# Two mixture-of-experts stages of a four-stage block: from every expert for every token to two experts per token, in blocks of 256 rows

## The reference, cut to what matters

```python
x = x + A(layernorm(x))   # linear attention: 16 heads of 8, a decayed scan over the tokens
x = x + B(layernorm(x))   # mixture: 8 experts of 352 hidden rows, the best 2 per token
x = x + C(layernorm(x))   # selective scan over the tokens, 16 states per feature
x = x + D(layernorm(x))   # mixture: 8 experts of 128 rows, best 2, and 2 shared experts
```

```python
out = sum over e of gate[t, e] * (silu(x @ W1[e].T) * (x @ W3[e].T)) @ W2[e].T
```

## Time and profile before

| | |
|---|---|
| median of 3 runs | 2572.25 us (2572.23 to 2573.89) |
| the profiled execution | 2568.12 us |
| its span, first to last instruction | 2566.3 us |
| mean granted TensorE clock | 0.907 of full speed |
| instructions | 22885 |
| DMA | 17.70 MB, mean 7 GB/s |

### The profile page before, as it was taken

How to read it: one execution, slowest core, us unless ns; L and a number is a source line. 1 busy time by engine, 2 the same in 40 slices (tenths; PEclk the granted TensorE clock), 3 DMA queues, 4 the chain that set the end, 5 groups by cost and what they waited for, 6 DMA issues and landing times.

```text
span 2566.3 us, 22885 instructions
## 1 busy us (share of the span) xinstructions
PE 2075.6 (81%) x6944; PEld 862.4 (34%) x6944; DVE 1855.6 (72%) x3076; ACT 1134.1 (44%) x1491; POOL 1347.3 (52%) x848
## 2 busy tenths in 40 slices
PE   3589787889788887799887997788877998787478
PEld 1234333334333343334333343333432433332023
DVE  5655569776796859867697767968598676974972
ACT  1133375335644275343752347442653437535324
POOL 4346347553573537735485445835377353862343
PEclk9789898899888999899988999889998999988579
DMA  4000000000000000000000000000000000000000
GB/s 131 0 9 1 9 1 1 0 1 17 0 1 0 1 17 1 0 1 1 17 0 1 1 11 7 1 1 1 17 1 1 1 1 9 1 0 1 0 0 17
DMA packets 24876, 17.70 MB, mean 7 GB/s; under 512 B 2705, under 2 KB 23985, under 8 KB 24497
## 3 DMA queue, kind: packets, MB, share of 16 engines
q1 hardware_dynamic: 24752, 16.23, 2.1%
HBM read 12.04 MB, written 4.19 MB: 6 GB/s over the span
## 4 chain that ended last, share of the span: by engine, by line
PE 42%; issue 20%; DVE 17%; POOL 13%; ACT 7%; DMA 0%; DVEq 0%; POOLq 0%; SPq 0%; ACTq 0%
PE bank L920 9%; PE bank L780 7%; POOL mix_arena L746 6%; PE bank L782 6%; PE bank L781 6%; POOL y L727 4%; DVE arena L1247 3%; DVE arena L1303 3%; PE bank L843 3%; PE bank L908 2%; PE bank L824 2%; PE bank L791 2%; DVE arena L1314 2%; POOL arena L717 2%; DVE w L1320 1%
## 5 line engine op out<-in xcount | busy, mean ns | idle before, releaser
L746 POOL TENSOR_TENSOR mix_arena<-mix_arena 128x512 f32<-128x512 f32 (+1 forms) x512 | 815.4, 1608 | 689.3 <-ACT mix_arena L1100 688.4
L1388 DVE SCALAR_TENSOR_TENSOR mix_arena<-bank,winv,mix_arena 128x512 f32<-128x512 f32 (+1 forms) x544 | 402.9, 743 | 421.8 <-PE bank L782 347.0
L1113 ACT ACTIVATE mix_arena<-bank,winv 128x512 f32<-128x512 f32 (+1 forms) x544 | 372.1, 687 | 540.2 <-PE bank L782 520.6
L920 PE MATMUL bank<-mix_arena,W_Bw 128*128 128x512 f32 (+1 forms) x768 | 437.8, 655 | 0.0
L727 POOL TENSOR_TENSOR y<-y,arena 128x1024 f32<-128x1024 f32 x120 | 284.2, 2368 | 184.1 <-DVE arena L1314 184.1
L1303 DVE TENSOR_TENSOR_SCAN arena<-arena 128x1024 f32<-128x1024 f32 x128 | 377.4, 2949 | 0.1
L780 PE MATMUL bank<-x_partsB,W_hi 128*128 128x512 f16 x712 | 298.3, 419 | 90.2 <-ACT mix_arena L1113 40.1
L1100 ACT COPY mix_arena<-bank 128x512 f32<-128x512 f32 x256 | 149.6, 584 | 480.1 <-PE bank L908 479.9
L876 PE MATMUL bank<-bc_parts,sel_bc 96*128 96x512 bf16 x512 | 197.2, 425 | 195.4 <-DVE arena L1314 149.9
L782 PE MATMUL bank<-x_partsB,W_lo 128*128 128x512 f16 x712 | 296.9, 417 | 0.0
L781 PE MATMUL bank<-x_partsB,W_hi 128*128 128x512 f16 x712 | 295.7, 415 | 0.0
(11 more groups left out here) (168 smaller groups left out, 2637.2 us busy)
## 6 DMA issues: line engine op xcount, KB each, us to landing
x<-in_x SPq DMA_DIRECT2D x8, 512.0 KB, 4.4
out<-x SPq DMA_DIRECT2D x8, 512.0 KB, 3.2
mix_arena<-in_W SPq DMA_DIRECT2D x2, 1408.0 KB, 8.7
W_Bw<-in_W SPq DMA_DIRECT2D x2, 512.0 KB, 14.1
mix_arena<-in_W SPq DMA_DIRECT2D x1, 640.0 KB, 11.3
x<-in_W SPq DMA_DIRECT2D x1, 640.0 KB, 12.4
W_Dw<-in_W SPq DMA_DIRECT2D x1, 640.0 KB, 4.7
x<-in_Wv SPq DMA_DIRECT2D x1, 512.0 KB, 5.3
```

The source lines that it names most:

```text
L746: pool.tensor_tensor(slot, slot, g_ring[0:rows, q % RG, :], ALU.mult).then_inc(m_sg[s].sem, 1)
L920: last = pe.matmul(banks[4][:], W2[s][0:rows, i, :], h_ring[0:rows, k % RH, :], start=(i == 0), stop=(i == NT[s] - 1))
L1113: read(s, act.activation(s_ring[0:rows, k % RS[s], :], bank(s, f"a{k}", rows), ACT.Silu, scale=down[W1[s]][0:rows]))
L1388: read(s, dve.scalar_tensor_tensor(out=h_ring[0:rows, k % RH, :], in0=bank(s, f"b{k}", rows), scalar=down[W3[s]][0:rows], in1=s_ring[0:row ...
```

## The change

Mixtures no longer compute every expert for every token. The names B, D, A and C of the stages stay, and the arithmetic of A and C does too. Per batch and mixture stage (a job q, 16 in all):

- **Prepare.** The rows are normalised as before, and ACT and POOL make the f16 high and low part of each row (`m_rows`), so that a row is 512 bytes. Logits and the best two are found as before (`m_choose`); then a count of tokens per expert ahead of each token is made by three small matmuls with a triangle and with ones (`m_rank`), and DVE works out a slot for each of the 2048 (token, expert) pairs, with every expert beginning at a multiple of 256, and a table of 15 experts, one per block (`m_place`).
- **Scatter.** POOL writes the rows to DRAM at their slots: 16 DMAs with an index list, each of 128 rows (`m_scatter`, four parts of four).
- **Blocks.** 15 blocks of 256 slots, whatever the choice of tokens is. For each, SP reads the expert from the table, loads its W1 and W3 parts and its W2 from DRAM (`load_weights`), and loads the 256 rows (`load_rows`). PE transposes them, multiplies (256 columns), and transposes the result back to rows, and SP stores them to DRAM. In B a block has three chunks of hidden rows, in D one.
- **Gather and add.** POOL fetches each token's two result rows with 16 more such DMAs (`m_gather`), and DVE adds them to x, times their gates (`m_combine`, 16 operations of 128 columns).
- **Shared experts** of D stay dense: four tiles of 512 columns (`m_shared`).

L746 (the gate multiplication on POOL), L908 and L1100 (spreading the gates), the accumulation over all tiles and the sum's transposes for B are gone; D keeps the transposes for the shared part. All of x now stays in SBUF. At the start the split weights are written to DRAM once (`keep`), W2 of B is copied within DRAM, and the four row buffers are filled with zeros.

The order comes from a plan: each step of each stage gets a time in units of a batch, the list is sorted, and each engine runs through it. C of batch b has the times b to b + 0.66 and A of batch b + 2 those from b + 0.67 to b + 1.

```diff
+    NB = 256
+    NBT = NB // P
+    BLOCKS = (2 * T + E * (NB - 1)) // NB
+    SLOTS = BLOCKS * NB
+    RW = {"B": 3, "D": 8}
+    R2 = {"B": 5, "D": 8}
+    LEAD = {"B": 2, "D": 5}
+    RX, XLEAD = 6, 3
...
+            if b >= 2:
+                put_attention(b, b - 2 + .67, b - 1, b - 2 + .5)
+                put_prep("B", b, b - 1 + .01, b - 1 + .23)
+                put_blocks("B", b, b - 1 + .25, b - 1 + .64)
+                put_combine("B", b, b - 1 + .67, .011)
+            put_prep("D", b, b + .67, b + .87)
+            for i, a in enumerate(spread(b + .85, b + .905, 6)):
+                put(a, "m_shared", b, i)
+            put_blocks("D", b, b + .915, b + 1.21)
+            put_combine("D", b, b + 1.235, .011)
...
+            def load_weights(q, k):
...
+                e = sp.value_load(table[0:1, q % RJ, k:k + 1], min_val=0, max_val=E - 1)
+                sp.dma_start(w13(s, k).rearrange("p w f -> p (w f)"),
+                             Wd[s][bass.ds(e, 1), :, :].rearrange("o p f -> p (o f)")).then_inc(w_in[m % RWL], 16)
+                sp.dma_start(w2(s, k).rearrange("p c d -> p (c d)"),
+                             W2d[s][bass.ds(e, 1), :, :].rearrange("o p f -> p (o f)")).then_inc(w_in[m % RWL], 16)
...
+            def m_scatter(q, part):
...
+                for i in range(part * TT // 2, (part + 1) * TT // 2):
+                    c, j = divmod(i, TT)
+                    pool.indirect_dma_start(
+                        out=xs_d[s, b % 2], out_offset=bass.IndirectOffsetOnAxis(ap=slot_idx[:, q % RJ, c, j:j + 1], axis=0),
+                        in_=xrow[:, j, :], in_offset=None, bounds_check=SLOTS - 1,
+                        oob_is_err=True).then_inc(scattered, 16)
...
+            def up_products(q, k, name, parts):
...
+                for i, (v, c) in enumerate(parts):
+                    f = slice(CHUNKS[s][c][0], CHUNKS[s][c][0] + CHUNKS[s][c][1])
+                    last = product(o[:, i * NB:(i + 1) * NB], wd[:, v, f], wd[:, v + 1, f], xh, xl)
+                filled(f"{name}{q}.{k}", last)
...
+            def m_combine(q, part):
...
+                    dve.scalar_tensor_tensor(out=x[:, b, j, :], in0=gath[:, c, j, :],
+                                             scalar=gate12[:, q % RJ, c, j:j + 1], in1=x[:, b, j, :],
+                                             op0=ALU.mult, op1=ALU.add).then_inc(added, 1)
```

1811 lines of the change are left out of this document (1013 added, 798 removed).

## The result

The changed kernel takes 2957.9 us (median of 4 runs, 2949.7 to 2960.9) where the one before takes 2572.2: a ratio of 1.150, 95% interval 1.147 to 1.153. The forecast was 2225, with a range up to 2600. It was wrong in sign and by 733 us.

The account below looks back on a forecast made before the run. The prediction had PE binding the attention phase and DVE and PE near their limit in C; head to 478, five periods of 240 (1200) and end 545 summed to 2223 us, some 2225 in all, range 2030 to 2600.

Parts of the forecast that it names:

- Bounds now: Before the change, PE binds the first 100 us of a 300.8 us period; DVE and PE are near their limit in the rest.
- PE's terms: PE's block products: 4.4 us per block of B, 2.0 of D; PE goes from 254 to about 200 us a period.
- DVE's terms: DVE's work: C phase 158.1 to 146 us, attention phase 70.5 to 63, with the scans getting shorter.
- rival 3: DVE fills up: stalls covered, scans fall to their minima, period 212, about 2040 us; chance 0.15.
- POOL's price: An indexed DMA holds POOL 1.64 us, 64 per period; POOL goes from 168 to 175 us, no bound.
- rival 1: POOL becomes the bound: an indexed DMA costs it 3.5 us, period 310, about 2770 us; chance 0.15.
- The cover of the bursts: Bursts of 16 indexed DMAs, 26 us each: C stalls 7 us twice; the attention phase is covered by the scan's lead.
- Rival 4: Latency of small steps: blocks wait for rows or weights and drag the scans; period 275, about 2470 us; chance 0.05.
- The idle time at the turns: Allowance beyond DVE's work: 14 us in the C phase, 17 at attention's start where PE, ACT and DVE take turns.
- Head and end: Outside the middle periods: the head from 143.89 us to the first scan stage takes 174 us, the end 545.
- The rule that speaks against it: Skill rule: a POOL DMA takes some 2.0 us plus bytes, 2.15 at 64 KB; all POOL's, the sum nears 2340.
- Rivals 1, 2 and 4: Rival 2 here: half-wide products cost as much as whole, period 287, about 2550 us, chance 0.07.

Follow-up runs that it names:

- run 35: Not a run's label: in "Over the whole run 35 start inside such a scan", 35 counts DMAs in the changed kernel's profile (2957.9 us).

## Why the prediction was wrong

The 733 us in order, each figure a difference of two measured kernels: 361 for the DMAs being indexed (2957.9 to 2596.5), 48 for what plain DMAs still hold of POOL's queue (to 2548.5), 55 for the shared bank (to 2493.1), 130 for the three parts of a block (to 2363.2; some of it is work that this kernel leaves out), and 138 between that and the forecast of 2225. The order of the steps has a part in how they share the loss, since causes overlap. The 138 were not taken apart by a run; what is known of them stands under the idle time at the turns and under the end.

**Bounds now.** Right, and the starting point of the error: near-full windows of a tuned period say which engine binds there, not how long the stage takes when that engine has less to do.

**PE's terms.** Right one by one. An f16 product of 256 columns starts every 0.11 us (0.12 taken), and the three f32 products that start at 1506.26 are followed by the next product at 1507.67, so 0.47 each (0.48 taken); the 1.56 us shown have a tail in them. PE has 202.8 us in a period where 200 was forecast, but that they agree so well has luck in it. At full clock a block of B takes 18 x 0.11 + 1.41 + 0.23 and 0.24 for its transposes = 3.9 us, where 4.4 was taken. The granted clock was 0.77 to 0.86, where the forecast had it full, and that goes the other way. From PE's timeline at 1501.62:
```profile
1501.62 0.27 PE L799 MATMUL bank<-xT_ring,mix 128*128 128x256 f16 x1
1501.73 0.27 PE L800 MATMUL bank<-xT_ring,mix 128*128 128x256 f16 x1
```

**DVE's terms.** Right in sum: 203.5 us against 209. The multiply of 256 columns is 0.478 (0.45); the addition of a row has a median of 0.341 (0.3), though its mean is 0.546 since some last up to 5.2 us. The scans fell to medians of 2.281 and 1.274 us, nearly to their minima, so rival 3's term for them came true, and it did not help, since DVE's idle time grew by 560 us in the same run. Duration (min/median/max ns) of the multiply and the addition:
```profile
L1530 DVE SCALAR_TENSOR_TENSOR mix<-bank,winv,mix x240: 443/480/486, 198.6 to 2912.6; 128x256 f32<-128x256 f32 x63, 96x256 f32<-96x256 f32 x57
L1558 DVE SCALAR_TENSOR_TENSOR x<-mix,gate,x x256: 319/341/5244, 319.7 to 2943.6; 128x128 f32<-128x128 f32 x128
```

**POOL's price.** I took 1.64 us for an indexed DMA; it holds POOL 0.97 to 1.01 when nothing is in its way and the next one starts 0.30 later, 1.3 in all. The mean over the run is 590 / 512 = 1.15, or 1.45 with the gap. POOL has 145 us in a period (175 forecast). The price was on the safe side. POOL is not full, so rival 1 did not come true, though the time lies on its side.

**The cover of the bursts: this is the step that failed first.** "In C a burst with its additions lasts about 30 us where the plan gives it 10, and two states of the ring cover some 13: a stall of 7 us, twice." The burst is 27 us where 26 was forecast. But the stall is 14.67 at the scatter alone, and straight behind it comes the gather; with the scan stretch at 148 us against 126 with plain DMAs, C loses 22 us, not 14. "In the attention phase the scan may run eight steps ahead, so the cover holds; if not, its PE products come late next" was the larger miss. The part from the end of C's scans to the next C takes 128.3 us, and 104.1 with plain DMAs, where the sum had no stall at all. The two windows with plain DMAs, attention's part and the scans:
```profile
1070.90:1175.00 104.10, 75.59 (x286) 35.86 (x286) 75.01 (x169) 31.18 (x54) 29.41 (x22) 0.85 0.21 59
1226.00:1352.00 126.00, 90.64 (x505) 62.18 (x506) 99.06 (x154) 63.26 (x98) 30.67 (x15) 0.80 0.41 120
```
In the changed kernel it goes like this. The gather of B runs from 1224.84 to 1247.32 on POOL, so that the first attention product L724 begins at 1249.41, 26.1 us after the start of attention (1223.3) and not 15.9 (1080.6 to 1096.5 with plain DMAs); the scatter of D runs from 1281.63 to 1305.64 with two of those products between its DMAs. DVE's timeline in this part has the waits in full:
```profile
1248.95 5.96 DVE L1558 SCALAR_TENSOR_TENSOR x<-mix,gate,x 128x128 f32<-128x128 f32 x4 [7.71 <-DMA mix<-outs,slot_idx]
1292.58 0.69 DVE L1333 TENSOR_TENSOR arena<-bank,z 128x512 f32<-128x512 f32 x1 [8.11 <-PE bank L800]
1301.64 0.75 DVE L1540 SCALAR_TENSOR_TENSOR mix<-bank,winv,mix 128x512 f32<-128x512 f32 x1 [7.18 <-ACT mix L1212]
1311.72 0.75 DVE L1540 SCALAR_TENSOR_TENSOR mix<-bank,winv,mix 128x512 f32<-128x512 f32 x1 [5.80 <-ACT mix L1212]
```
7.71 us for gathered rows, 8.11 for an attention product (the lead of eight steps ran out), 7.18 and 5.80 for the shared expert, whose products stand in PE's queue behind those that wait for POOL: 28.8 us, where the same waits come to 2.2 with plain DMAs. That is the 24, and a little more. So the bursts cost 22 + 24 = 46 us a period where the sum had 14.

**The blocks costed at DVE's share.** In the sum a block cost what DVE has to do for it: 1.19 us in B and 0.45 in D, 25 us a period. Measured, seven blocks of each stage fewer shorten the period by 29.1 us (293.0 to 263.9, from the gates y times z at 774.3 and 2239.5, and at 685.3 and 2005.0), so 2.1 us for each where DVE's share had 0.8 on average. If each of the 30 costs that, they cost 62 (an estimate). Rival 4 (period 275, 2470), held at 0.05, named half of this mechanism: each block "drags the scans behind it in every in-order queue". Its other half, that a block waits for rows or weights, did not come: without the wait for rows 20 us come back. I let it stand as an alternative to the bursts; it came on top of them.

**The idle time at the turns.** 14 us in the C phase and 17 at the start of attention were allowed. The windows of the earlier trace rows would have told: DVE idles for 30 us of the 100 and for 42 of the 200.36 before the change. I read the second as mutual waiting that goes when there is less work. The finer windows above show that 20.2 of it is the head of C, and in the kernels whose period is cut that way here it is never under 19.7. With the attention part the two are 62 us before and 49 to 59 in the kernels with plain DMAs, where the sum had 31.

**Head and end.** C of batch 0 begins its convolution at 382.8, not 318 (318.63 before). With plain DMAs it is 339.0, with 8 blocks besides 293.2: both causes are there in full, since little lies beside the blocks of B0. From the last attention to the end it is 2947.6 - 2242.8 = 704.8 us where 545 was forecast, of which 125.6 is the last stage D (145 forecast). With plain DMAs the same stretch takes 586.6 us and with 8 blocks besides 517.9, so the same two causes are in it. But one term of the sum was wrong by itself. Between the end of the second last C and the convolution of the last one stood 30 us of "gather, addition and normalising"; it takes 95.0:
```profile
2569.80:2664.80 95.00, 41.40 (x175) 24.56 (x174) 32.88 (x130) 23.00 (x41) 40.04 (x38) 0.62 0.22 63
```
The gather of B (2581.77 to 2602.73) is there as forecast, but the plan puts stage D's preparation, its scatter (2624.51 to 2644.77) and its first six blocks ahead of C too, and no attention runs beside them. With plain DMAs it is still 66.2 us (2239.5 to 2305.7).

**SP and DMA at nothing.** Right. No wait of PE for weights appears; the first rows of a stage are waited for (135.7 us), and without that wait only 20 us come back.

**The rule that speaks against it.** In C's stretch above, the DMAs that start while a scan of 1024 elements runs last 2.22 to 3.00 us and end 0.78 to 0.88 after the scan. One of them: 1403.32 + 2.74 = 1406.06, the scan ends at 1405.28. Over the whole run 35 start inside such a scan (one of them within 0.01 us of its start); they last 1.92 to 3.13 us, and every one ends 0.77 to 0.90 us after the scan does. One more, that started 0.08 us ahead of a scan, lasted 3.20 and ended 0.84 after it. The others have a mean of 1.03. The Trainium skill, "SBUF — State Buffer", section "SBUF: two separate sides", says that POOL and a DVE operation that takes both ports, or one with two inputs in SBUF against a POOL operation that reads SBUF, shut each other out until the first is done, and tells of a DMA from POOL of 0.62 us that takes 3.1. The trace agrees for indexed DMAs, but for the end: the Trainium skill has it 0.12 us after DVE's, here it is 0.8. The plain ones were not held: the longest of 512 is 0.864 us though they run beside the same scans. A scan is here the second kind of operation, with two inputs in SBUF, and for that kind the rule asks for an operation of POOL that reads SBUF. The index list lies in SBUF, so only an indexed DMA has something to read there, and the rule would fit both; no run shows that this is the reason. I had put this rule under rival 1 with a price for POOL's throughput; its 35 cases are worth some 60 us of POOL's time and by themselves explain little of 361.

The other rule is that of the Trainium skill, "DMA: Bandwidth & Descriptors", section "Anatomy of one DMA — SWDGE (gpsimd) path": some 2 us for a DMA of POOL, most of it completion. For a plain one the trace agrees: it holds POOL 0.54 us and lands 2.2 us after its issue (median of the gathers). An indexed one holds POOL 1.0 us, 1.3 with the gap, and the trace does not have its landing, so how much of its time is not POOL's is not shown. Had the 2.15 us all been POOL's, the sum was 2340, and it would still have missed by 600.

**The chances.** Slower had 0.19, and the range ended at 2600. Rivals 1, 2 and 4 were each worked out with all other terms of the forecast in place. None had the burst's cover and the blocks' cover fail together, which is what happened. Rival 3 has a slip: from a period of 240 to 212 are 28 us, so its time was about 2030 and not 2040.

## What to carry to other kernels

When a change takes work from the busiest engines, do not scale the stage with it: cut the profile of before into windows at every change of stage, take the busiest engine's idle time in each, and keep most of that time: here 62 us at the turns became 49 to 59 in kernels with much less work. Price a new burst in an in-order queue by the first thing that stands behind it at the place where it stands, not by the load of the engine: at 40% load, four fifths of what was taken out of POOL's queue came out of the time. And cost a small step that hops between four engines by its hops: blocks whose share of the fullest engine is 0.8 us on average cost 2.1, and here its hops showed their worth only when they were shortened together.
